# Self-attention steps: turnings, output projections and the gate's products of neighbour batches moved to other key tiles

## What is computed

```
h = rms(x, w_ln1)
q, k, v = h @ wq + bq, h @ wk + bk, h @ wv + bv      # 16 heads of 32
q, k = rope(q, k)
attn = softmax(causal(q @ k.T * 32 ** -0.5))
x = x + (attn @ v) @ wo
h = rms(x, w_ln2)                                    # goes to the router and the experts
logits = h @ w_router
```

## Time and profile before

| | us |
|---|---|
| median of 3 runs | 2431.61 |
| the three runs | 2431.61, 2431.66, 2427.66 |
| profiled execution, its own time | 2428.34 |
| its span | 2426.4 |
| mean granted TensorE clock | 0.996 |
| TensorE busy | 2338.6 |
| VectorE busy | 1347.1 |
| ScalarE busy | 1340.5 |
| GpSimd busy | 919.1 |

### The profile page before, as it was taken

The page is one execution under the profiler, slowest core; times in us unless marked ns, Lnnn a source line. Parts: engine busy times, 40 slices in busy tenths (PEclk is TensorE's granted clock), DMA queues, the critical chain, the costliest instruction groups (busy, mean ns, idle before and its releaser), DMA issues. The chain is left out here.

```text
span 2426.4 us, 38547 instructions
## 1 busy us (share of the span) xinstructions
PE 2338.6 (96%) x15120; PEld 1498.5 (62%) x15120; DVE 1347.1 (56%) x2102; ACT 1340.5 (55%) x1695; POOL 919.1 (38%) x610
## 2 busy tenths in 40 slices
PE   9999999999999999999999899999899999999998
PEld 7887444444444444444334556666578899998886
DVE  6677434443444434434522666565675577777785
ACT  4333577667767777767897433533522256665222
POOL 2238564655456544655302333333024112221320
PEclk9999999999999999999999999999999999999999
DMA  6003775567546763667642400002045357776431
GB/s 226 18 18 120 215 203 120 148 175 200 127 117 165 202 180 87 156 180 203 170 110 76 157 1 1 19 1 73 24 134 182 109 186 268 252 254 205 149 104 53
DMA packets 205490, 326.68 MB, mean 135 GB/s; under 512 B 71264, under 2 KB 126048, under 8 KB 205152
## 3 DMA queue, kind: packets, MB, share of 16 engines
q1 hardware_dynamic: 185952, 246.51, 36.3%
q0 software_dynamic: 16336, 72.23, 9.0%
q10 hardware_dynamic: 3024, 5.51, 0.7%
HBM read 238.39 MB, written 96.27 MB: 138 GB/s over the span
## 5 line engine op out<-in xcount | busy, mean ns | idle before, releaser
L1110 ACT ACTIVATE A_c_prob<-c_psum 128x1024 f32<-128x1024 f32 x832 | 786.8, 1029 | 280.5 <-PE c_psum L1367 274.7
L1037 POOL TENSOR_TENSOR E_c_roots<-E_c_roots,c_half 128x32 f32<-128x32 f32 (+1 forms) x70 | 363.2, 5190 | 402.2 <-DVE E_c_roots L1127 402.1
L1376 PE MATMUL c_psum<-A_c_prob,c_vq 128*17 128x512 f32 x3328 | 414.7, 598 | 8.6 <-DVE c_oT L1267 8.3
L143 PE MATMUL c_psum<-E_c_w,E_c_c 128*128 128x512 f32 x1248 | 312.6, 400 | 1.6 <-DVEq L1252 0.7
L143 PEld LDWEIGHTS c_psum<-E_c_w,E_c_c 128*128 128x128 f32 x1248 | 226.6, 188 | 122.8 <-issue 41.0
L1367 PE MATMUL c_psum<-c_qq,c_kq 64*128 64x512 f32 x1664 | 285.5, 435 | 15.0 <-ACT A_c_prob L1110 9.9
L1367 PEld LDWEIGHTS c_psum<-c_qq,c_kq 64*128 64x128 f32 x1664 | 135.6, 184 | 158.1 <-ACT A_c_prob L1110 84.0
L1166 DVE COPY E_c_unit<-c_psum 128x256 f32<-128x256 f32 x89 | 37.8, 425 | 328.3 <-PE c_psum L143 328.3
L2772 PE MATMUL m_psum<-A_m_dn_hi,A_m_a 128*128 128x512 f32 (+1 forms) x576 | 187.9, 394 | 4.2 <-DVE A_m_a L2510 4.2
L1376 PEld LDWEIGHTS c_psum<-A_c_prob,c_vq 128*17 128x17 f32 x3328 | 68.6, 96 | 188.4 <-issue 165.2
L143 PE MATMUL m_psum<-R_g_hi,U_s_up 128*128 128x512 f32 x528 | 170.0, 395 | 0.6 <-DVEq L2491 0.6
(11 more groups left out here) (360 smaller groups left out, 3954.4 us busy)
## 6 DMA issues: line engine op xcount, KB each, us to landing
c_kq<-kd SPq DMA_DIRECT2D x248, 208.0 KB, 6.0
kd<-S_c_t SPq DMA_DIRECT2D x96, 256.0 KB, 4.0
E_c_raw<-in_ctxT SPq DMA_DIRECT2D x89, 256.0 KB, 4.4
qd<-A_c_q SPq DMA_DIRECT2D x64, 256.0 KB
c_qq<-qd SPq DMA_DIRECT2D x64, 256.0 KB, 3.1
vd<-A_c_vt SPq DMA_DIRECT2D x104, 136.0 KB, 3.6
c_vq<-vd SPq DMA_DIRECT2D x31, 442.0 KB, 8.8
S_up_raw<-in_sup SPq DMA_DIRECT2D x20, 512.0 KB, 4.6
```

The costliest lines, as they stand in the source:

```text
L143: mm = pe.matmul(out, a(c), b(c), start=first and i == 0, stop=last and i == len(terms) - 1)
L1037: pool.tensor_tensor(rr[:, unit % RB, 0:n], ms[:, unit % RB, 0:n], half[:, 0:n], ALU.pow).then_inc(s_r, 1)
L1110: act.activation(prob[:, t % PB, 2 * (u % 2):2 * (u % 2) + 2, :], score_banks[u % 3], ACT.Exp, scale=XD ** -0.5).then_inc(s_ex, 1)
L1376: mm = pe.matmul(o_bank[32 * j:32 * j + VW, :], vq[:, q % 2, kt, j, :], prob[:, t % PB, j, :], start=kt == 0, stop=kt == CT - 1)
```

## The change

It edits the lists and VectorE's order.

- Second step of a batch (c = 1): H(b+1,2) and H(b+1,3) go from `late` to `early` of tile 2. O(b-1,0) goes from `early` of tile 3 to `late` of tile 2 (batches 1 and 2), or to `early` of tile 2 (batch 3, which has no H). O(b-1,1) stays in tile 3.
- Third step of the last batch (step 14): O(2,2) and O(2,3) go from tiles 2 and 3 to tiles 0 and 1, the four G(0,k) from tiles 0 and 1 to 2 and 3.
- R(0) and L(0) go from `late` of tiles 2 and 3 of step 14 to `early` of tiles 0 and 1 of step 15, and G(1,k) from tiles 0 and 1 to 1 and 2 of step 15.
- VectorE: the maximum comes ahead of the items in every tile; an O in a step's last tile is taken behind the step's reciprocal and product (`behind`).

The number and shape of all instructions stay.

```diff
@@ -1463,20 +1463,26 @@
                     early.append(self.item("V", b, 2 + kt // 2))
                 if n == 0 and kt == 1:
                     early.append(self.item("V", 0, TT - 1))
-                if c == 1 and kt == 3 and b:
-                    early += [self.item("O", b - 1, t) for t in range(2)]
-                if c == 2 and kt >= 2 and b:
+                if c == 1 and kt == 2 and b + 1 < B:
+                    early += [self.item("H", b + 1, 2 + k) for k in range(2)]
+                if c == 1 and kt >= 2 and b and (kt == 3 or b == B - 1):
+                    early.append(self.item("O", b - 1, kt - 2))
+                if c == 2 and b and kt >= 2 and b < B - 1:
                     early.append(self.item("O", b - 1, kt))
+                if c == 2 and kt < 2 and b == B - 1:
+                    early.append(self.item("O", b - 1, 2 + kt))
                 if c == 3 and kt >= 2 and b + 1 < B:
                     early.append(self.item("V", b + 1, kt - 2))
-                if c == 1 and kt in (1, 2) and b + 1 < B:
-                    late += [self.item("H", b + 1, 2 * (kt - 1) + k) for k in range(2)]
-                if n == self.N - 2 and kt < 2:
-                    early += [self.item("G", 0, 2 * kt + k) for k in range(2)]
+                if c == 1 and kt == 1 and b + 1 < B:
+                    late += [self.item("H", b + 1, k) for k in range(2)]
+                if c == 1 and kt == 2 and b and b + 1 < B:
+                    late.append(self.item("O", b - 1, 0))
                 if n == self.N - 2 and kt >= 2:
-                    late.append(self.item("RL"[kt - 2], 0, 0))
+                    early += [self.item("G", 0, 2 * kt - 4 + k) for k in range(2)]
                 if n == self.N - 1 and kt < 2:
-                    early += [self.item("G", 1, 2 * kt + k) for k in range(2)]
+                    early.append(self.item("RL"[kt], 0, 0))
+                if n == self.N - 1 and kt in (1, 2):
+                    early += [self.item("G", 1, 2 * kt - 2 + k) for k in range(2)]
                 self.early[n].append(early)
                 self.late[n].append(late)
             if n + 1 < self.N:
@@ -1845,19 +1851,14 @@
                     dve.wait_ge(s_wrhi, 1)
                     dve.tensor_tensor(wr_lo, wr, wr_hi, ALU.subtract).then_inc(s_wr, 1)
                 for kt in range(TT):
-                    outputs = c == 1 and kt == TT - 1
-                    if outputs:
-                        for item in line.early[n][kt]:
-                            take(item)
                     if n + 1 < STEPS:
                         maximum(n + 1, TT - 1 - kt)
                     if kt == 0 and n:
                         low_output(n - 1)
-                    if not outputs:
-                        for item in line.early[n][kt]:
+                    behind = [item for item in line.early[n][kt] if item.kind == "O" and kt == TT - 1]
+                    for item in line.early[n][kt] + line.late[n][kt]:
+                        if item not in behind:
                             take(item)
-                    for item in line.late[n][kt]:
-                        take(item)
                     if n == 1:
                         norm.statistics(kt)
                         if kt == TT - 1:
@@ -1875,6 +1876,8 @@
                     dve.reciprocal(a[:], sum_bank).then_inc(s_rec, 1)
                     dve.wait_ge(s_rec, n + 1)
                     dve.tensor_tensor(a[:], o_bank, a[:], ALU.mult).then_inc(s_a, 1)
+                for item in behind:
+                    take(item)
 
             def last_low(t):
                 ts = slice(t * P, (t + 1) * P)
```

## The result

The changed kernel took 2447.0 us (median of 4 runs, 2446.0 to 2450.2) against 2429.6 before (4 runs): ratio 1.0071, interval 1.0059 to 1.0083, so 0.7% slower. The forecast was 2446 in 2436 to 2454. The profiled execution is the slowest of the four, 2450.2 us with a span of 2447.5, 21.1 us more than before. From T(0) to the turnings behind step 15 it took 416.0 us (1341.8 to 1757.8) against 400.2 (1340.0 to 1740.1): **15.8 of the 21.1 us lie in the sixteen steps.** Of the other 5.3 us, 1.8 lie ahead of the steps and 3.5 behind them. They are partly the clock in code that didn't change: the granted clock was 0.66 from 1785 to 1790 and 0.67 from 2080 to 2085, where before had no such fall.

What follows compares the result with a forecast made beforehand. TensorE, busy 2338.6 of 2426.4 us, was taken as the bound, so its gaps were summed: stalls 12.5 less gains 0.6 and 0.9 make 11.0, plus clock 5.5, on 2429.8, gives 2446 us, range 2436 to 2454.

Steps and rivals of the forecast that it cites:

- The stalls: Start of steps 6, 7, 10, 11, 14: TensorE stands 3.25 us each for an output's bank; four outside the last batch, 12.5 us.
- The clock: Behind the stalls: TensorE's granted clock falls, 1.4 us each; four of five falls taken, 5.5 us.
- Rival 1: The stalls come but the clock holds at full: 2441 us, chance 0.28.
- The early turnings: Steps 1, 5, 9, with the late output in 5 and 9: gain 0.3 us a step, 0.6 for two; step 1 nothing.
- The last batch: Steps 13 to 15: TensorE's waits go from 9.8 to 8.9 us, gain 0.9, stall included.
- the fourth tile of step 15: Last tile of step 15: wait of 0.7 + 0.8 us, the exponential late by some 0.8 behind ScalarE's G and normalising.
- The sum: Whole kernel: waits 11.0 plus clock 5.5 make 16.5 us more, 2446 us.
- Rival 3: Stalls beget others: all clock falls come, plus a further microsecond per stall from a late maximum; 23 us, 2453 us, chance 0.12.

Runs made afterwards that it cites:

- Experiment 1: Changed kernel with no output behind the division (VectorE takes maximum, output, then reciprocal): 2423.5 us, ratio 0.9968 to the kernel before.
- experiment 2: Kernel before, with only the last output of the third step put behind the division in batches 1 and 2: 2439.3 us, ratio 1.0032.
- experiment 4: Changed kernel with the delayed output taken between the reciprocal and the product instead of behind the product: 2441.6 us, ratio 1.0038.
- experiment 7: Kernel of Experiment 1 with the lists of steps 13 to 15 as in the kernel before: 2430.7 us, ratio 1.0005.
- experiment 8: Kernel before, with only VectorE's order changed, maximum ahead of the two outputs in the second step's last tile: 2434.1 us, ratio 1.0016.

## Why the prediction was right, step by step

- **The stalls: right.** T + 5.2 was forecast for the bank, T + 5.21 is A's start; five places, as listed. The view of waits shows 3.05 to 3.07 each, since it does not count the 0.2 us between two starts. Steps 6 and 7, from ScalarE's copy of one turning to the next, grew by 4.8 and 4.3 us, that is 3.25 and 2.99 of stall (0.26 swallowed at step 7) and the clock. Experiments 1, 2 and 4 took away all stalls, put in two, and shortened all, and the time followed by 23.5, 8.5 and 5.4 us (24.6, 8.5 and 6.5 against their own times before).
- **The clock: right in kind, a little small.** Four falls of five were taken, 5.5 us. The profiled execution has all five; 4.8 - 3.25 and 4.3 - 2.99 are 1.5 and 1.3 us each, and filling the stalls gave 5.8 us back (6.9 against its own time before). The reason given for four, that part of a slow spell can lie in the stall itself, does not show in this execution. (At step 11 of experiment 2 it does: the clock fell some 1.4 us before the stall's end, and yet that fall cost 2.3.) All five falls begin at the end of the stall or behind it: at step 7 the product starts at 1525.82 at full clock, and the fall comes some 1 us later.

```profile
1524.00:1527.00 3.00, 1.18 (x5) 1.01 (x6) 1.73 (x3) 2.61 (x6) 0.00 (x0) 0.99 0.00 0
1527.00:1530.00 3.00, 3.00 (x14) 1.74 (x12) 0.00 (x0) 0.00 (x0) 0.00 (x0) 0.50 0.00 0
```

Rival 1, the clock that holds, was wrong. The Trainium skill, "TensorE: Matmul & The Clock Gate", section "HAM oscillation — how this bites in real kernels", ties a fall to an idle gap longer than any of these. The traces differ from it: the clock fell behind five gaps of 3.05 to 3.07 us in this kernel and behind four of five of 2.3 in experiment 4.

- **The early turnings: right, and small.** Waits of 0.45 and 0.99 on the turned input's low parts were forecast as 0.59 + 0.2 and 1.05; step 5 became 0.46 us shorter, 0.3 had been forecast. (By the prediction's own times, 1480.10 and 1481.07, the last of the three is 0.97 and not 1.05.) What it left out is that the steps behind 5 and 9 grow, by 0.4 in experiment 7, so that hardly anything of the 0.6 is left where no stall hides it.
- **The last batch: the gain was mis-sized.** "Sum 8.9: gain 0.9, stall included" was too little (its terms add up to 8.8). From step 13 on the waits of the changed kernel are 0.33, 0.32, 3.06, 0.54, 0.44, 0.22, 0.33, 0.88, 0.17, 0.23, 0.87 and 0.57, together 8.0, or 8.2 with the stall counted as 3.25: a gain of 1.6 on the 9.8 of the earlier trace rows. By the times from ScalarE's copy of T(13) to the end of step 15 (69.2 us with a fall of 1.4 in it, 70.3 before) it is 2.5. Experiment 1, without the stall, has 64.4 there and so gains some 6, where 0.9 + 3.25 had been forecast: 1.8 too little. Part of that is in no wait of the list, and what it is stays open. The term that was most off among the waits is the fourth tile of step 15: 0.7 + 0.8 was forecast, and 0.87 measured. ScalarE does take two G and two normalised rows between two exponentials, but TensorE's G products and sums cover nearly all of it:

```profile
1753.57 1.26 ACT L1696 ACTIVATE R_g_hi<-s_psum,S_w 128x512 fp32r<-128x512 f32 x2
1754.71 1.34 ACT L1683 ACTIVATE A_s_xs<-A_s_xs,s_rr 128x512 f32<-128x512 f32 x2
1755.93 0.60 ACT L1736 ACTIVATE A_s_pT<-s_psum 128x512 f32<-128x512 f32 x1
```

- **The sum.** 16.5 was forecast, 17.4 measured (interval 14 to 20), so the two mis-sized terms nearly cancel: the last batch gives 0.7 to 1.8 more, the clock takes 0.3 to 1.5 more. That the sum came within 1 us of the time is in part luck. Rival 3's further microsecond for each stall was not seen.

## What to carry to other kernels

Where buffers go round in turn, an item's release is a deadline of the item two places on: before one engine's release is put behind a long instruction (here a reciprocal of 3.35 us), count on to the next user of that bank and read how soon it comes. Here a stall of 2.3 us or more on TensorE cost its length and then, nearly always, a clock fall that cost 1.3 to 2.7 us more, so a short stall that can't be avoided is worth filling with idle products if a free bank is at hand. And an order that looks wasteful on one engine (outputs ahead of the maximum) may be what frees a bank in time; try it alone, as in 8, before it is dropped.

## What the runs showed of the hardware

I had not expected that gaps this short would be followed by falls so often: five of five at 3.06 us of idleness, and two of two in experiment 2; four of five at 2.28; none of five where the gap was filled down to 0.43. Behind each of the five there are three microseconds with a granted clock of 0.50 (from 1496.5, 1527, 1609, 1640 and 1718.5), so the clock was at 1.2 instead of 2.4 GHz for all of them. A fall cost 1.3 to 1.5 us at steps 6 and 7, but 2.3 at step 11 of experiment 2 and 2.7 at step 10 of experiment 4, where it lasted longer. Single waits of 1.54 us are followed by falls at two of four places: steps 6 and 10 of experiment 8, but not its step 14, nor that of experiment 7. In batch 0 the clock falls one to three times in every other profiled execution, not always at the same places (1342 and 1366 before; 1343 and 1411 after the change), behind several short waits among small products; with these filled the one profiled execution had none. Why a given one falls and another does not stays open.
